# A third x2 slot, and the even tile's second LayerNorm issued in the middle of the pair before it

## The reference, cut to what matters

```python
x = x + attention(layernorm(x))                  # called x2 in the kernel
h = layernorm(x)                                 # "LN2", gives h0
for blk in range(3):
    y = h @ dequant(q[2*blk]).T + bias + lora    # Y1
    y = layernorm(y) * gamma + beta              # L1
    y = gelu(y)                                  # Ga
    y = y @ dequant(q[2*blk+1]).T + bias + lora  # Y2
    h = y + h                                    # E2
out = x + h
```

## Time and profile before

| | |
|---|---|
| median of 2 runs | 4063.06 us (4062.56 to 4063.55) |
| the profiled execution's own time | 4065.35 us |
| its span, slowest of 8 cores | 4063.8 us (all cores 4051.6 to 4063.8) |
| phase A, weights, phase B (from the span's start) | 0 to 2048, 2048 to 2177, 2177 to 4064 us |
| TensorE busy | 2492.2 us, 61% of the span |
| VectorE busy | 1981.5 us, 49% |
| ScalarE busy | 1009.9 us, 25% |
| GpSimd busy | 77.0 us, 2% |
| issue of y's store at the end of pairs 0 to 7 | 2416.34, 2648.49, 2882.23, 3116.99, 3352.97, 3588.89, 3824.05, 4059.36 us |

### The profile page before, as it was taken

One profiled execution on the slowest core, in us unless ns is written; L12 is line 12 of the kernel. 1 busy time (PEld: TensorE's weight loads), 2 busy tenths in 40 slices (PEclk: granted clock), 3 DMA queues, 4 the chain that ended last, 5 costly groups with the idle time before them and its releaser, 6 DMA issues.

```text
span 4063.8 us, 57513 instructions; the slowest of 8 cores (4051.6 to 4063.8 us)
## 1 busy us (share of the span) xinstructions
PE 2492.2 (61%) x20161; PEld 1592.6 (39%) x20176; DVE 1981.5 (49%) x3863; ACT 1009.9 (25%) x1729; POOL 77.0 (2%) x126
## 2 busy tenths in 40 slices
PE   0566765666656566666534756658485766757666
PEld 0344433444443344444311534435253434434343
DVE  0455544545544454554424555545455554545454
ACT  0122333222323322233354212212121221212121
POOL 1000000000000000000011000000000000000000
PEclk9767666777776677776556878878797887878788
DMA  9012111111111111111232010010102011010101
GB/s 140 14 29 32 25 29 30 31 30 31 24 35 30 30 31 29 31 25 35 31 95 70 1 53 1 22 32 1 52 1 52 1 26 27 6 47 1 52 1 32
DMA packets 259705, 128.18 MB, mean 32 GB/s; under 512 B 229232, under 2 KB 233504, under 8 KB 259424
## 3 DMA queue, kind: packets, MB, share of 16 engines
q1 hardware_dynamic: 228864, 79.72, 9.6%
q0 software_dynamic: 30560, 44.79, 5.9%
HBM read 61.99 MB, written 25.17 MB: 21 GB/s over the span
## 4 chain that ended last, share of the span: by engine, by line
PE 44%; DVE 25%; ACT 10%; issue 9%; DMA 5%; another core or an unknown queue 2%; DVEq 2%; SPq 1%; ACTq 1%; POOL 0%; POOLq 0%
PE psA L1265 11%; PE psB L1442 5%; PE psA L1442 4%; DMA arena<-arena 4%; ACT arena L794 3%; PE psA L772 3%; PE psA L1271 2%; PE psA L384 2%; DVE arena L1346 2%; DVE arena L806 2%; PE psA L459 2%; PE psB L891 2%; ACT arena L1399 2%; ACT L1354 2%
## 5 line engine op out<-in xcount | busy, mean ns | idle before, releaser
L1265 PE MATMUL psA<-arena,wbig 128*128 128x256 bf16 x3072 | 468.5, 303 | 0.5 <-DVEq L1294 0.2
L772 PE MATMUL psA<-arena 64*128 64x256 bf16 x960 | 251.3, 392 | 169.5 <-ACT arena L794 169.4
L1265 PEld LDWEIGHTS psA<-arena,wbig 128*128 128x128 bf16 x3072 | 296.5, 107 | 117.5 <-issue 32.8
L806 DVE TENSOR_TENSOR arena<-arena,mlocS 128x512 bf16<-128x512 bf16 x480 | 204.1, 425 | 228.2 <-ACT arena L794 204.3
L1354 ACT ACT_TABLE_LOAD x48 | 61.6, 1283 | 1008.9 <-DVEq L1347 1008.9
L1291 DVE TENSOR_SCALAR arena<-psA,biasS 128x256 bf16<-128x256 f32 x384 | 185.9, 484 | 243.6 <-PE psA L1271 201.6
L794 ACT ACTIVATE arena<-psA 128x512 bf16<-128x512 f32 x480 | 261.4, 595 | 59.4 <-PE psA L772 58.3
L1442 PE MATMUL psA<-arena,wbig 128*128 128x256 bf16 x1536 | 219.7, 290 | 0.0
L384 PE MATMUL psA<-wbig,arena 128*128 128x512 bf16 x497 | 131.7, 425 | 134.2 <-DMA arena<-arena 120.9
L1442 PE MATMUL psB<-arena,wbig 128*128 128x256 bf16 x1536 | 201.1, 274 | 0.0
L772 PEld LDWEIGHTS psA<-arena 64*128 64x128 bf16 x960 | 73.4, 107 | 319.6 <-issue 310.2
(11 more groups left out here) (166 smaller groups left out, 4266.7 us busy)
## 6 DMA issues: line engine op xcount, KB each, us to landing
y<-arena SPq DMA_DIRECT2D x16, 1024.0 KB, 4.3
arena<-qT POOLq DMA_DIRECT2D x48, 256.0 KB, 2.6
arena<-x_in POOLq DMA_DIRECT2D x16, 512.0 KB, 7.4
x2scr<-arena SPq DMA_DIRECT2D x16, 512.0 KB, 3.5
arena<-x2scr POOLq DMA_DIRECT2D x16, 512.0 KB, 6.0
arena<-arena SPq DMA_TRANSPOSE x224, 3.2
wbig<-wq POOLq DMA_DIRECT2D x1, 2048.0 KB, 17.8
wbig<-wk POOLq DMA_DIRECT2D x1, 2048.0 KB, 29.1
```

The costliest lines, as they stand in the source:

```text
L772: mm = t.matmul(reg[:, hh * 256:(hh + 1) * 256], ar_t.ap()[0:64, o_KR + h * 2 * W + sl * W + koff: o_KR + h * 2 * W + sl * W + koff + 128] ...
L806: v.tensor_tensor(dst.rearrange("p (g q) -> p g q", g=2), dst.rearrange("p (g q) -> p g q", g=2), mkv, op=ALU.mult)
L1265: t.matmul(reg, wTv(i0, c, oc * 128, 128), V(hin_o + c * TILE, TILE), start=(c == 0), stop=False)
```

## The change

The arena gets a third x2 slot, `o_x2t3`; tile tj uses slot tj mod 3, and its load waits for the tail three tiles back instead of two, and for the landing of the load before it that counts on the same semaphore. `emit_ln2_h0` is split into `emit_ln2` (VectorE and ScalarE) and `emit_h0` (the transposes on SP). The load and LN2 of the next pair's even tile are now written in block k = 1 of the pair before, between `b_L1e(B, 1)` and `b_Ga(A, 1)`; its `emit_h0` stays at the pair's end. The odd tile's load, LN2 and h0 stay there too.

```diff
+        o_x2t3 = Bv(NCH * TILE)
...
+        X2SLOT = lambda tj: (o_x2t + (tj % 3) * NCH * TILE
+                             if tj % 3 < 2 else o_x2t3)
+
         def emit_x2load(tj):
...
-                if tj >= 2:
-                    g.wait_ge(ve.h, ve_after_x2[tj - 2])
+                if tj >= 3:
+                    g.wait_ge(ve.h, ve_after_x2[tj - 3])
+                g.wait_ge(dx2l[pj].h, dx2l[pj].n)
                 I(dx2l[pj], g.dma_start(
-                    V(o_x2t + pj * NCH * TILE, NCH * TILE).rearrange("p (tc f) -> p tc f", tc=QC),
+                    V(X2SLOT(tj), NCH * TILE).rearrange("p (tc f) -> p tc f", tc=QC),
...
-        def emit_ln2_h0(tj):
+        def emit_ln2(tj):
...
             ln2_done_d[tj] = ve.n
+
+        def emit_h0(tj):
+            pj = tj % 2
 
             @block.sync
             def _(sy, tj=tj, pj=pj):
...
                     b_L1e(Bst, k)
                 else:
                     b_L2(A, k)
+                if k == 1 and 2 * pair + 2 < nbt_total:
+                    emit_x2load(2 * pair + 2)
+                    emit_ln2(2 * pair + 2)
                 b_Ga(A, k)
                 b_Y2(A, k)
                 b_E2(A, k)
...
             b_tail(Bst)
-            for tj in (2 * pair + 2, 2 * pair + 3):
-                if tj < nbt_total:
-                    emit_x2load(tj)
-                    emit_ln2_h0(tj)
+            if 2 * pair + 2 < nbt_total:
+                emit_h0(2 * pair + 2)
+            if 2 * pair + 3 < nbt_total:
+                emit_x2load(2 * pair + 3)
+                emit_ln2(2 * pair + 3)
+                emit_h0(2 * pair + 3)
```

More of the change, by code:

```diff
@@ L1107, in _ @@
                     g.wait_ge(dx2s.h, dx2s.n)
-                if tj >= 2:
-                    g.wait_ge(ve.h, ve_after_x2[tj - 2])
+                if tj >= 3:
+                    g.wait_ge(ve.h, ve_after_x2[tj - 3])
+                g.wait_ge(dx2l[pj].h, dx2l[pj].n)
                 I(dx2l[pj], g.dma_start(
-                    V(o_x2t + pj * NCH * TILE, NCH * TILE).rearrange("p (tc f) -> p tc f", tc=QC),
+                    V(X2SLOT(tj), NCH * TILE).rearrange("p (tc f) -> p tc f", tc=QC),
                     x2_dram[bj, Tj * TILE:(Tj + 1) * TILE, :].rearrange(
                         "(tc p) f -> p tc f", p=128)), 16)
-        def emit_ln2_h0(tj):
+        def emit_ln2(tj):
             pj = tj % 2
-            x2vj = V(o_x2t + pj * NCH * TILE, NCH * TILE)
+            x2vj = V(X2SLOT(tj), NCH * TILE)
             ve_stats2 = {}
@@ L1181, in build_program @@
                 emit_x2load(1)
-            emit_ln2_h0(0)
+            emit_ln2(0)
+            emit_h0(0)
             if nbt_total > 1:
-                emit_ln2_h0(1)
+                emit_ln2(1)
+                emit_h0(1)
         Y1BANKS = ['A0', 'A0', 'A1', 'A1']
@@ L1199, in b_state @@
                 ti=ti, b=b, T=T, pp=pp, q0=T * TILE,
-                x2v=V(o_x2t + pp * NCH * TILE, NCH * TILE),
+                x2v=V(X2SLOT(ti), NCH * TILE),
                 y1F=(o_y1F if pp == 0 else o_t1F),
```

## The result

The changed kernel took 4136.42 us (median of 11 runs, 4129.96 to 4241.49), the kernel before, timed beside it, 4065.98 us (10 runs). The ratio is 1.018 with a 95% interval of 1.0145 to 1.0216: slower, by some 73 us, where 77.6 were forecast. Timed again beside a later group of experiments, the changed kernel had a median of 4134.22 us.

A forecast was written before the change was run, and what follows sets the result against it. The prediction took the kernel as one long hand-over between engines, with TensorE's standstills deciding. Seven pairs lose 13.6 us each (95.2), boundaries gain 17.6, net 77.6: 4063.06 to 4140.7 us, own range 4131 to 4148, overall 4112 to 4158.

The forecast's parts named there:

- The Gelus lose their cover: Middle of the pair: tile A's block 1 Gelus wait for LN2's second root, so TensorE starts Y2 13.0 us later.
- The clock adds 0.6: Y2 of tile A, block 1: TensorE restarts at its lower clock after the stall, adding 0.6 us a pair.
- The boundary gains 2.3, and 3.8 at the last: Between pairs: h0 transposes issue 6.16 us earlier but meet store and load; gain 2.3 us, 3.8 where no load is left.
- Third slot, added wait, odd tile: Third x2 slot, added semaphore wait, split function and the odd tile's early x2 load were to cost nothing.
- Sum: Whole kernel: 95.2 us lost, 17.6 gained, net 77.6 slower, 1.9% more, to 4140.7 us.
- The transposes that meet nothing: Rival at the boundary: transposes gain the full 6.16 us at seven boundaries, 52.1 us slower, 4115; chance 0.09.
- The late transposes: Rival at the boundary: transposes move only once the load has landed, gain 0.8 us, 4152.7; chance 0.24.
- The dearer table switch: Rival on ScalarE: the bare root-to-Gelu switch costs another 1.28 us, 9.0 in all, 4149.7; chance 0.05.
- The clock paid back: Rival: the rest in the middle gives later TensorE starts full clock, some 12 us a pair back, 4057; chance 0.04.

The follow-up runs named there:

- e2_ln2_behind_gelu: Changed kernel with the even tile's load and LN2 written behind the Gelus of tile A, block 1, instead of ahead; ratio to before 1.010, 4104.1 us.
- e3_wait_only: Kernel before with one wait exchanged: Gelus of tile A, block 1, wait for tile B's squares, no LN2 moved; ratio 1.0154, 4123.59 us.
- e8_after_again: The changed kernel itself, nothing altered, timed again in a later group; ratio to before 1.0127, median 4134.22 us.
- e1_slots_only: Changed kernel with the even tile's load and LN2 written back at the pair's end; ratio to before 1.0015.
- e7_overlap: Changed kernel, even tile's LN2 and h0 moved into tile B's block 2, next Y1 put ahead of B's output addition and store; ratio to before 0.9794, 4001.97 us.
- e11_no_load: Changed kernel with the even tile's x2 load held on POOL until Y1 of tile A has run, store still ahead; ratio to before 1.011, 4116.22 us.
- e4_store_behind_h0: Changed kernel with the even tile's h0 transposes ahead of tile B's y store in SP's queue; ratio to before 1.0141.
- e10_no_store_no_load: Changed kernel with h0 transposes ahead of the y store and the x2 load held until Y1 of tile A has run; ratio to before 1.0101, 4113.6 us.
- e9_overlap2: As e7_overlap, with the lora part of the odd tile's Y1 ahead of tile B's output addition; ratio to before 0.9726, 3964.5 us.

## Why the prediction was right

*The Gelus lose their cover, 13.0 us a pair.* Measured 12.91 in the row and 91.0 / 7 = 13.0 in the sum. e2_ln2_behind_gelu shows that ScalarE's order is the cause, e3_wait_only how much of it is coupling.

*The clock adds 0.6.* This term was mis-sized. Y2 behind the new stall takes 11.93 us in the row and 12.0 in the mean of all 56 of e8_after_again (seven a core), against 11.99 warm. The slow start is there, but the new Y2 saves something that the two Y2 the term was taken from save too and the warm one doesn't: its first chunk doesn't wait 1.4 us for the lora copy, since VectorE is idle by then. In those two the slow start outweighed this by 0.4 and 0.8; here the slow part is shorter, only the first two groups of eight (1.86 and 1.67), and it comes out even. Besides, some of TensorE's later work in the pair is faster than before: Y1b(A, 2) and Y1b(B, 2), the next two long stages, take 11.2 and 11.2 us in the mean instead of 11.5 and 11.7. In the table the rest of a pair grows by 0.7, with 1.4 of wait gone: together -0.7 where +0.6 was forecast, which is 9 us in seven pairs.

*The boundary gains 2.3, and 3.8 at the last.* Measured 20.32 - 18.33 = 2.0 at the boundary shown, 17.0 us in sum against 17.6. At the last, where no load is left, the gap is 15.8, some 4.4 less than before. The reason given, that the transposes queue behind a store and a load, was tested by taking each away: 2 us for each. The picture was somewhat too neat, though: the transposes do not simply wait for the store and then run at their own speed; their issue on SP is itself drawn out, from 2.6 us to 4.2 behind the store and 6.2 with the load besides. The Trainium skill (DMA: Bandwidth & Descriptors, "Queues, rings and completion order") has the descriptors of one row consumed in ring order on each engine. The runs agree: the transposes gained 2 us when the store was put behind them. By the same section an engine takes packets in turn from the rows that have work. That agrees too: the load, in another row, holds the transposes 2 us.

*Third slot, added wait, odd tile: nothing.* e1_slots_only shows no price, within its interval.

*Sum.* 91.0 - 17.0 - 10 = 64 from the waits and 7 x 0.7 = 5 from slower work make 69; the ratio says 73 (59 to 88), and 77.6 were forecast. The clock term is the difference; the stall and the boundary came out as forecast.

*The rivals.* The transposes that meet nothing would need gaps of 14; they appear only with store and load removed. The late transposes would need gaps of 19 and more. The dearer table switch did not occur: 0.02 us between root and table load in the exposed place too. The Trainium skill (ScalarE: Activation LUTs, "What ACT_TABLE_LOAD costs") counts a drain of 1.38 us to each switch. The trace does not agree: no such time stands in this chain. The clock paid back no more than those tenths, not the 11.1 us a pair of that rival. Whether the change lies within 2% of no change is not settled, since the interval of 1.0145 to 1.0216 reaches beyond it; the forecast of 1.9% had put it just inside, and that is a matter of sizes, not of mechanism.

## What to carry to other kernels

Before moving work into another stage's shadow, ask for each engine's queue what stands behind the moved instructions, and what that had been hidden under: here two activations of 0.2 us, written ahead of eight Gelus, tied one tile's path to the other's and made a stall of 13 us a pair. The right shadow is one in which the bounding engine waits for the same queue anyway; the same work in that place cost 1 us. And a DMA that is issued earlier meets other traffic: look at the DMA share in the stretch that it moves into before counting the whole distance as gain. And count what TensorE does behind a wait, not only the wait: in e7_overlap 3.5 of the 12.7 us that each pair saved in waits came back as longer work.

## What the runs showed of the hardware that was not expected

- Behind a 1 MB store in the same queue, two DMA transposes take 4.2 us to issue on SP instead of 2.6, and land in 3.9 to 5.1 us instead of 3.2 (e11_no_load). With a 512 KB load of another queue in flight besides, the issue takes 6.2 us and they land in 6.0 to 7.4 (changed kernel). With that load and the store behind them, the issue takes 2.7 us and they land in 5.7 to 6.0 (e4_store_behind_h0). With neither in the way, they land in 3.2 (e10_no_store_no_load).
- The prices of the store and of the load on the path were 2 us each and added up: mean gaps of 18.0 with both, 16.0 and 16.1 with one, 14.0 with neither.
- Behind a wait of only 3.9 us TensorE can run at half its clock, while behind the wait of 1.4 us in e9_overlap2 the next eight matmuls still take 1.05 us. The windows of the first such wait in e7_overlap show it; the first of each row's last three numbers is the granted clock. It is still 1.00 (2.4 GHz) while TensorE waits, falls as its work begins again, stays at 0.50 (1.2 GHz) and is back after some 6 us of work:

```profile
3090.00:3092.00 2.00, 0.00 (x0) 0.00 (x0) 1.41 (x4) 0.20 (x1) 0.00 (x0) 1.00 0.00 0
3092.00:3094.00 2.00, 0.41 (x3) 0.32 (x4) 1.38 (x4) 0.00 (x0) 0.00 (x0) 0.62 0.19 39
3094.00:3096.00 2.00, 2.00 (x10) 1.06 (x9) 0.57 (x2) 0.00 (x0) 0.00 (x0) 0.50 1.04 196
3096.00:3098.00 2.00, 2.00 (x10) 1.03 (x9) 0.00 (x0) 0.00 (x0) 0.00 (x0) 0.50 0.14 27
3098.00:3100.00 2.00, 2.00 (x12) 1.24 (x11) 0.97 (x2) 0.00 (x0) 0.00 (x0) 0.67 0.00 0
3100.00:3102.00 2.00, 2.00 (x18) 1.34 (x16) 0.70 (x2) 0.00 (x0) 0.00 (x0) 1.00 0.00 0
```
